# Second layer's cross attention: scores from stacked high and low parts of queries and keys, laid out by DMA

## The reference

```python
def _L1_xattn_ref(q, k, v, Wq, bq, Wk, bk, Wv, bv, Wo, bo):
    HEADS, D_MODEL, D_K = 16, 256, 16
    B, LQ, _ = q.shape
    LKV = k.shape[1]
    qh = (q @ Wq + bq).reshape(B, LQ, HEADS, D_K).transpose(0, 2, 1, 3)
    kh = (k @ Wk + bk).reshape(B, LKV, HEADS, D_K).transpose(0, 2, 1, 3)
    vh = (v @ Wv + bv).reshape(B, LKV, HEADS, D_K).transpose(0, 2, 1, 3)
    scores = jnp.einsum('bhqd,bhkd->bhqk', qh, kh) * (1.0 / np.sqrt(D_K))
    attn = jax.nn.softmax(scores, axis=-1)
    out = jnp.einsum('bhqk,bhkd->bhqd', attn, vh)
    return out.transpose(0, 2, 1, 3).reshape(B, LQ, D_MODEL) @ Wo + bo
```

## Time and profile before

| | us |
|---|---|
| three runs | 1852.93, 1856.81, 2038.5 |
| median | 1856.81 |
| profiled execution: its own time | 1852.35 |
| profiled execution: span from first to last instruction | 1850.7 |
| PE busy | 1370.4 (74%) |
| DVE busy | 1043.4 (56%) |
| ACT busy | 500.6 (27%) |
| POOL busy | 438.0 (24%) |
| mean granted clock of TensorE | 0.839 |

### The profile page before, as it was taken

The page is one execution under the profiler, slowest core; times in us unless marked ns, Lnnn a source line. Parts: engine busy times, 40 slices in busy tenths (PEclk is TensorE's granted clock), DMA queues, the critical chain, the costliest instruction groups (busy, mean ns, idle before and its releaser), DMA issues.

```text
span 1850.7 us, 24852 instructions
## 1 busy us (share of the span) xinstructions
PE 1370.4 (74%) x8316; PEld 984.7 (53%) x8316; DVE 1043.4 (56%) x2199; ACT 500.6 (27%) x1196; POOL 438.0 (24%) x519
## 2 busy tenths in 40 slices
PE   3676775666667599962659878599686797776988
PEld 1554554454464366641448755378453686544865
DVE  5355445436536233327766676666667665876654
ACT  2231222222223122211224312244113343132430
POOL 1141052134025200016422112221112321032210
PEclk8796687688679699985779979699897799997999
DMA  9300010065002311111200000000000000000000
GB/s 377 154 10 1 1 55 6 0 264 225 0 16 101 130 46 46 46 35 47 87 0 2 17 1 11 1 1 17 1 10 1 1 17 1 1 10 1 2 1 9
DMA packets 22248, 81.17 MB, mean 44 GB/s; under 512 B 3692, under 2 KB 7788, under 8 KB 20592
## 3 DMA queue, kind: packets, MB, share of 16 engines
q1 hardware_dynamic: 16496, 68.88, 9.9%
q0 software_dynamic: 5632, 10.77, 2.0%
HBM read 40.10 MB, written 39.52 MB: 43 GB/s over the span
## 4 chain that ended last, share of the span: by engine, by line
issue 44%; PE 29%; POOL 12%; DVE 9%; POOLq 2%; ACT 2%; DVEq 2%; DMA 1%; SPq 0%; ACTq 0%
PE ps L913 6%; PE ps L1133 4%; PE ps L932 3%; PE ps L1141 2%; POOL headbd L595 2%; PE ps L508 2%; POOL experts L1415 2%; POOL bd_hi L611 2%; PE ps L451 2%; POOL bd_lo L611 1%; PE ps L459 1%; POOL xn L494 1%; POOL small L408 1%; POOL tok_d L1387 1%; DVE x L1963 1%
## 5 line engine op out<-in xcount | busy, mean ns | idle before, releaser
L1318 ACT ACTIVATE probs<-ps,small 100x361 f32<-100x361 f32 x256 | 141.4, 558 | 194.9 <-DVE small L1924 194.9
L1924 DVE TENSOR_REDUCE small<-ps 100x2 f32<-100x722 f32 x128 | 116.0, 908 | 105.5 <-PE ps L960 105.5
L595 POOL TENSOR_TENSOR headbd<-kT,cst 128x800 f32<-128x800 f32 x64 | 97.4, 1525 | 194.8 <-DVE kT L1812 117.1
L433 PE MATMUL ps<-cst,xn 100*128 100x100 f32 x256 | 50.8, 351 | 121.4 <-DVE xn L397 83.6
L508 PE MATMUL ps<-headbd,qT 128*100 128x400 f32 x256 | 116.8, 539 | 20.0 <-POOL headbd L595 15.3
L913 PE MATMUL ps<-every,xT_t 128*128 x256 | 122.3, 601 | 0.4 <-issue 0.4
L1133 PE MATMUL ps<-hT,experts 128*128 128x400 f32 x288 | 117.8, 560 | 1.2 <-DVE small L628 1.2
L1084 PE MATMUL ps<-cst,probs 100*121 100x100 f32 x768 | 104.8, 273 | 12.4 <-ACT probs L1318 12.4
L958 PE MATMUL ps<-k_hi,bd_hi 128*100 128x362 f32 x256 | 103.6, 405 | 10.2 <-DVE bd_lo L611 10.2
L433 PEld LDWEIGHTS ps<-cst,xn 100*128 100x128 f32 x256 | 35.7, 197 | 138.6 <-DVE xn L397 85.2
L1084 PEld LDWEIGHTS ps<-cst,probs 100*121 100x121 f32 x768 | 97.3, 189 | 20.6 <-issue 7.8
(11 more groups left out here) (297 smaller groups left out, 2890.6 us busy)
## 6 DMA issues: line engine op xcount, KB each, us to landing
tok_d<-wt SPq DMA_DIRECT2D x1, 14848.0 KB, 45.8
res_d<-wt SPq DMA_DIRECT2D x1, 14848.0 KB, 48.9
every<-e_d SPq DMA_DIRECT2D x8, 1536.0 KB, 18.3
ctxT<-ctxT_d SPq DMA_DIRECT2D x8, 726.0 KB, 5.0
x_t<-tok_d POOLq DMA_DIRECT2D x32, 128.0 KB, 2.4
res_d<-out_t SPq DMA_DIRECT2D x32, 128.0 KB, 1.7
experts<-e_d SPq DMA_DIRECT2D x1, 3456.0 KB, 10.7
wt<-w_d SPq DMA_DIRECT2D x1, 3134.0 KB, 13.8
```

The costliest lines, as they stand in the source:

```text
L595: inc(e.tensor_tensor(headbd[:, u % 2], keysT[:, c, b * S:(b + 1) * S].unsqueeze(1).broadcast_to([P, HC, S]), cs("head").unsqueeze(2).broa ...
L1318: ins = e.activation(f_e[:, n % 2, i, 0:LC], bank(2 * (n % 2) + i, S, LC), ACT.Exp, bias=h_nm[:, n % 2, i:i + 1], accum_out=h_sum[:, b, h: ...
L1924: inc(e.tensor_reduce(h_nm[:, n % 2, 0:2], ps[0:S, 2 * (n % 2):2 * (n % 2) + 2, 0:LC], AX, ALU.max, negate=True), "F_nm")
```

## The change

Stage F's scores use a stack instead of block diagonals. Of a head's contraction, 48 rows are used (`PART`): its 16 query rows as (high, high, low) against the key rows as (high, low, high), which is the sum of the three products. Two heads lie one above the other in 96 partitions; the query stack is zero in the other head's half. So a unit's scores are two matmuls, one per head.

- Queries: `q_stack` [96, 16 heads, 400] in the scratch area. POOL clears it once, behind its 24 gathers. SP copies each of a chunk pair's 8 heads three times per half, 24 DMAs of 16 partitions x 2 chunks x 200 columns (`stack_queries`): 16 from `q_hi` after `F_qT`, 8 from `q_lo` after `F_ql`.
- Keys: `k_stack[c]` [96, 4, 362] for chunk c, one buffer each, in the places of the block diagonals. SP stores `k_hi` and `k_lo` of the chunk to DRAM (`key_d`, double buffered), waits until both have landed, waits that the last scores of this chunk of the sequence before are done (`F_s`), and loads six DMAs of 16 partitions x 4 x 362 (`stack_keys`).
- Order on SP (`feed`): keys of sequence 0, queries of both halves, keys of sequences 1 to 3, then the next group's context and the result's store.
- PE waits for `key_in[c]` at every fourth unit and for `query_in` at the first unit of each half.
- POOL's block diagonals of the stage and DVE's two for the first sequence go.
- The five `kv` steps, and the copies of keys and values that follow them, move two units forward (from v = 3..7 to 1..5).
- The first three expert loads share one (PE's first three tiles wait for all three), and `r_diffs` is merged into `r_tiles`, which the same engine counts right beside it.

```diff
+PART = 3 * HD
...
-        values_ = sb("values_", [P, 2 * VU + 8192])
+        values_start = -(-nc.sbuf_base // 32) * 32
+        values_ = sb("values_", [P, NVU * VU + NH * NT])
...
-        bd_hi = nc.alloc_sbuf_tensor_at("bd_hi", [P, 2, HC, S], F32R, offset=headbd_start)
-        bd_lo = nc.alloc_sbuf_tensor_at("bd_lo", [P, 2, HC, S], F32R, offset=bdx_start)
+        q_stack = nc.alloc_sbuf_tensor_at("q_stack", [2 * PART, NH, NT], F32R, offset=values_start + 4 * NVU * VU)
+        k_stack = [nc.alloc_sbuf_tensor_at(f"k_stack{c}", [2 * PART, HC // 2, LE], F32R, offset=o)
+                   for c, o in enumerate((bdx_start, headbd_start))]
...
+            def stack_keys(g, b, c):
+
+                n = 2 * b + c
+                W(e, "F_kv", g, 5 * b + c + 1)
+                for j, k in enumerate((k_hi, k_lo)):
+                    e.dma_start(key_d[n % 2, j], k[:, b % 2, c, :].bitcast(F32)).then_inc(key_out.sem, 16)
+                e.wait_ge(key_out.sem, key_out.free(g, 32 * (n + 1)))
+                e.sem_inc(key_kept.sem, 1)
+                if b >= 1:
+                    W(e, "F_s", g, 8 * (b - 1) + 4 * (c + 1))
+                for i in range(2):
+                    for j, k in enumerate((0, 1, 0)):
+                        o = PART * i + HD * j
+                        e.dma_start(k_stack[c][o:o + HD].bitcast(F32), key_d[n % 2, k].rearrange(
+                            "(p i d) n -> i d p n", i=2, d=HD)[i]).then_inc(key_in[c].sem, 16)
+
+            def stack_queries(g, h):
+
+                for j, q in enumerate((q_hi, q_hi, q_lo)):
+                    if j == 0:
+                        W(e, "F_qT", g, 1, h)
+                    if j == 2:
+                        W(e, "F_ql", g, h + 1)
+                    for i in range(HC):
+                        o = PART * (i % 2) + HD * j
+                        dst = q_stack[o:o + HD].rearrange("p (c i) n -> p c i n", c=DC)[:, :, i, tok(h)]
+                        e.dma_start(dst.bitcast(F32), q[HD * i:HD * (i + 1), :, tok(h)].bitcast(F32)
+                                    ).then_inc(query_in[h].sem, 16)
+
+            def feed(g):
+
+                stack_keys(g, 0, 0)
+                stack_keys(g, 0, 1)
+                stack_queries(g, 0)
+                stack_queries(g, 1)
+                for b in range(1, NB):
+                    stack_keys(g, b, 0)
+                    stack_keys(g, b, 1)
+
+            e.wait_ge(q_blank.sem, 1)
             with e.Fori(0, NG - 1) as g:
+                feed(g)
                 W(e, "F_kvp", g, 5 * NB)
...
-                        e.wait_ge(ld_e0[t].sem, 16)
+                        e.wait_ge(ld_e0[t].sem, 48 if t < 3 else 16)
...
-                    W(e, "F_bd", g, 2 * b + c + 1)
-                    if b == 0:
-                        W(e, "F_bl", g, c + 1)
-                    if v == 0:
-                        W(e, "F_kv", g, 5 * b + 2)
+                    if v % 4 == 0:
+                        e.wait_ge(key_in[c].sem, key_in[c].free(g, 96 * (b + 1)))
+                    if v == 0 and b % HB == 0:
+                        e.wait_ge(query_in[b // HB].sem, query_in[b // HB].free(g, HC * 48))
...
-                        ins = product(bank(2 * (n % 2) + i, S, LE), (bd_hi[:, c, h, :], bd_lo[:, c, h, :]),
-                                      k_hi[:, b % 2, c, :], k_lo[:, b % 2, c, :], True, True)
+                        ins = e.matmul(bank(2 * (n % 2) + i, S, LE), q_stack[:, c * HC + h, b * S:(b + 1) * S],
+                                       k_stack[c][:, h // 2, :], start=True, stop=True)
...
-                    if n < len(units) and b + 1 < NB and 3 <= v < 8:
-                        kv(g, b + 1, v - 3)
+                    if n < len(units) and b + 1 < NB and 1 <= v < 6:
+                        kv(g, b + 1, v - 1)
...
+            e.memset(q_stack[:].bitcast(F32), 0.0).then_inc(q_blank.sem, 1)
...
-                for b in range(NB):
-                    own_q = slice(b * S, (b + 1) * S)
...
-                        for dst, q in ((bd_hi, q_hi), (bd_lo, q_lo))[:2 if b else 1]:
-                            ins = over_heads(e, dst, q, b, c)
-                        inc(ins, "F_bd")
...
-                        if b + 1 < NB and v in (4, 5):
-                            key_lo(g, b + 1, v - 4)
+                        if b + 1 < NB and v in (2, 3):
+                            key_lo(g, b + 1, v - 2)
...
-                    if n < 8 * NB and b + 1 < NB and v >= 5:
-                        value_evac(g, b + 1, v - 5)
+                    if n < 8 * NB and b + 1 < NB and 3 <= v < 6:
+                        value_evac(g, b + 1, v - 3)
```

More of the change, by code:

```diff
@@ L737, in _ @@
                 e.sem_inc(x_free.sem, 1)
+            feed(NG - 1)
             W(e, "G_acc", NG - 1, E1)
@@ L954, in _ @@
             tile_down(NTILE - 1, before)
-            def product(out, w, rhs_hi, rhs_lo, start, stop):
-                wh, wl = w
-                e.matmul(out, wh, rhs_hi, start=start, stop=False)
-                e.matmul(out, wh, rhs_lo, start=False, stop=False)
-                return e.matmul(out, wl, rhs_hi, start=False, stop=stop)
             def ternT_pe(g, h, j, b0):
@@ L2066 @@
     scratch = [nc.dram_tensor(n, (ROWS, D), F32, kind="Internal").ap() for n in ("tok_d", "res_d")]
-    decoder(nc, *aps, out, *scratch)
+    keys = nc.dram_tensor("key_d", (2, 2, P, LE), F32, kind="Internal").ap()
+    decoder(nc, *aps, out, *scratch, keys)
     r = run_bass_kernel_spmd(nc, [arrays], core_ids=[0])
```

33 lines of the change are left out of this document (12 added, 21 removed).

## The result

The changed kernel takes 1880.7 us (median of four executions, 1878.4 to 1880.9) against 1854.9 for the kernel before, measured beside it: a ratio of 1.0142, with an interval of 1.0122 to 1.0162. It is slower by 1.4%, 26 us. One of the four executions of the kernel before took 2038.5 us and is left out of the ratio. The forecast of 1848 had the wrong sign; the time lies inside the range of 1825 to 1885, near its upper end. The profiled execution has a span of 1876.7 us against 1850.7.

The account below looks back on a forecast made before the run. It took stage F to be bound by PE's work and, almost equally, a PE-DVE-ACT-PE round trip, the latter after the change; 1852.35 - 56 (loop) + 42 (query copies) + 4 (clock) + 6 (clear) = 1848.3 us, range 1825 to 1885.

Parts of the forecast that it names:

- The work saved in the loop: Stage F's 32-unit loop: undisturbed units fall from 2.45 to 2.12 us, saving 14.0 per group, 56 in all.
- The loop about 79 us long: Sign to look for: stage F's loop of 32 units lasts about 79 us, where group 0 took 93.4 before.
- I take 0.47: Start of stage F: SP issues query copies 0.47 us apart, so PE starts 10.5 us later per group, 42 in all.
- 24s - 0.8: Start of stage F: stall in us per group before the first scores, with s the spacing of SP's issues.
- Just in time, by 1.5: Second sequence's keys in stage F: ready at 30.3 us after the queries' release, wanted by the ninth unit at 31.8.
- 32s - 16.5: Ninth unit of stage F: lateness in us of the second sequence's keys, with s the spacing of SP's issues.
- 56s + 4: Stage F: us from the queries' release until the second sequence's keys have landed, with s SP's issue spacing.
- SP's issue is the bound: Stage F, slower: at a spacing of 0.76, stall 17.4 and late keys 7.8 per group, 1907 us in all; chance 0.14.
- Issue is cheap: Query copies in stage F, faster: spacing 0.06, stall 0.6 per group, 1805 us in all; chance 0.09.
- The clock falls inside the loop: Stage F's loop, slower: a quarter of the time at PE's lower clock, 46 us more, 1894 in all; chance 0.07.
- A thirteen-microsecond pause makes the first units run at the lower level: First units of stage F's loop: PE at 1.2 GHz after the pause, 1 us per group, 4 in all.
- The clear: POOL's one clear of the stacked queries before group 0's first key diagonal: takes 5.9 us, 6 on the path, bounds 3 to 6.

Follow-up runs that it names:

- the run with late keys: Version with queries through DRAM, its kv steps and the copies behind them moved back to v = 3 to 7: 1860.0 us, ratio 1.0026 to the kernel before.

## Why the prediction was wrong, point by point

**The work saved in the loop: right.** Forecast were undisturbed units at 2.12 in pairs and 19.0 for a block with keys; measured are 2.44 and 1.81 in turn, and 19.09. The loop does not run at 1.80, PE's own work: in these units PE waits 0.4 us for ACT's exponentials in every second one, which fits the round trip PE, DVE, ACT, PE read from the earlier trace rows. The forecast of 14.0 per group, 56 in all, agrees with the run without the copies: its total is 50 us lower with the clear's 6 paid, 56 in all, the slow first units included. "The loop about 79 us long" did not come: the changed kernel's loops keep 35 of the 56, and the late keys and slow first units below take the rest.

**"I take 0.47": the step that failed.** It came from bigger copies from DRAM, and the prediction said that none like the new ones is in the trace. The new ones, from SBUF to SBUF, are issued 0.645 apart. With that in the prediction's own terms, 24s - 0.8 is 14.7 per group and not 10.5; measured are 14.0, 13.9, 13.9 and 13.7 more from release to first scores, 55 in all instead of 42. The landing term of 2.0 was right (1.9). The mechanism, scores that wait for a string of 24 issues on SP, was right; its size was not. The bound of 0.76 held the value, but the choice went to the row of the same engine that lay nearest, though source, size and shape were other. With 24 to 56 copies to multiply it, the upper bound deserved more of the chance.

**"Just in time, by 1.5": failed with it, and was too cheap besides.** 32s - 16.5 is 4.1 late at 0.645. PE waited for the keys 0.3, 2.5, 3.1 and 0.4 us in the four groups. The keys landed 39.8 to 41.2 us after the release, as 56s + 4 says at 0.645 (40.1); but PE came to the ninth unit 21.4 to 23.1 us after its first scores and not after 18.5, so that it waited less. Yet compared with the intervals of the version through DRAM the late keys cost 3.9, 5.7, 6.3 and 0.5: 16.4 us. The formula has the same total at four times 4.1, but by luck: it overstates the wait and leaves out the clock, which makes 2.5 us of waiting cost 5.7. The prediction's sum had put the late keys at nothing.

**The rivals.** *SP's issue is the bound* was the right mechanism, at s = 0.645 just under the 0.68 where it passes +2%: in its terms 14.7 + 4.1 + 1 - 14.0 = 5.8 per group, and with the 6 for the clear 1852.35 + 23.3 + 6 = 1881.6, against 1878.4 of the profiled execution and 1880.7 of the median. That the two agree so well is in part the luck just named. It had a chance of 0.14, where the sign of the result hung on s being above 0.51 (there 24s - 0.8, with 1 for the clock and 1.5 of the clear per group, reaches 14.0), only 0.04 from the value taken. *Issue is cheap* fell: an issue for the queries takes 0.38 to 0.65 us on SP and 0.50 to 0.51 on POOL in these traces, and 24 in a row take 15.5 us where a copy lands after 1.9. The Trainium skill ("DMA: Bandwidth & Descriptors", on the anatomy of one DMA, there one that POOL issues) puts sequencer dispatch at about 50 ns. No whole issue in these traces is that short, neither on SP, to which the prediction applied the figure, nor on POOL. *The clock falls inside the loop* came in another form than described: not from gaps of 0.3 us in each unit (undisturbed blocks keep the pace of the full clock), but in the first units of each group and behind three of the four late keys. Over the loops alone, from first scores to last maximum, the granted clock is 0.85, 0.88, 0.88 and 0.91. The prediction had named a clock under 0.95 as a sign that it is wrong, and so it was.

**"A thirteen-microsecond pause makes the first units run at the lower level": half right.** At the start of a loop PE runs at the lower level for 9 to 13.5 us (3.4 before), and the first seven intervals take 18.3 to 20.0 us, against 17.1 to 17.3 where the clock is at its best (three groups of the run with 14 matmuls in the pause). That is 1 to 3 us per group, as the term had it. But the length of the pause explains little of it: without the copies, where scores begin 2.9 us after the release, the lower level still holds for 7 to 13 us of the loop. What else sets it, the lighter work of the first units for one, was not run by itself.

**The clear: right.** 5.9 for it and 6 on the path were forecast, 5.45 and 6.3 measured. What no step foresaw is that taking it off again gains nothing in the end.

**The moved `kv` steps.** The prediction treated their shift as neutral. The run without it shows that it is worth 32 us in the version through DRAM, through keys in time and through what it changes in the first block together.

**Sum.** 1848.3 + 13 (spacing at the start) + 16 (late keys, with what the clock adds) = 1877; the profiled execution, from which the forecast started, took 1878.4, and the median is 1880.7.

The queries' way through DRAM beats both kernels: 0.9865 of the kernel before, 2.8% less than the changed kernel.

## What to carry to other kernels

Before work is given to DMA, count the issues on the way to the first consumer and multiply by a spacing measured for that kind of copy: 24 small copies are 15.5 us of one engine's time here, copies of half the size cost as much each, and one or two large trips through DRAM can be shorter. Then look at what stands behind them in the same queue; an idle engine's queue may be the cheapest gain (42 us against the changed kernel, together with copies in the order of use). And on an engine that is at its limit, a short wait inside a dense loop can cost twice its length or more (16.4 us for 6.4 of waiting here), because the clock may fall behind it.

## What was not expected of the hardware

- Time per DMA in a string of issues on SP: 0.645 us from SBUF to SBUF (0.63 with one dimension less, 0.73 for the clear of 96 partitions), 0.45 from DRAM to SBUF. A store from SBUF to DRAM takes 0.36 to 0.43 us to issue. On ACT the SBUF copies took 0.64 too, on POOL 0.51. That the source in SBUF is the cause is inferred from copies of different shapes; the same copy with only its source changed was not run.
- A wait of 2.55 us on PE was followed by 10.2 us at the lower clock level (six transposes 1.38 instead of 0.88), and so was one of 0.28 in group 0; waits of 0.41 in group 3 and of 1.76 in the run with late keys were followed by none. The first two or three intervals of each group are slow the same way (5.8, then 2.7 to 4.4 us), whether scores begin 16.8 or 2.9 us after the release.
- At the start of phase three 5.8 us were gained in the changed kernel and 4.7 in the version through DRAM; 1.5 and 0.3 us of the span were left, with the granted clock of the same late stretch at 0.83 instead of 0.89.
